# Static zero rows ahead of each pair's region, the last tile read from further back, and the imaginary product on VectorE

## The reference, cut to what matters

```python
# x: (8, 1024, 128) float32: 8 batches of 1024 tokens with 128 features
x = x + attn(layernorm(x))
x = x + moe(layernorm(x))

def attn(x):
    h = layernorm(x, gamma, beta)
    h = spiral_conv(h)          # Re(conv(h, p^t * init) + last * p^(t+1)), p one complex number per feature
    x1 = h + x
    h = layernorm(x1, gamma, beta)
    return silu(h @ w1 + b1) @ w2 + b2 + x1      # w1 128x512, w2 512x128

def moe(x):                     # 8192 tokens, 8 experts, 2 chosen for each token
    logits = x @ router.T
    top, idx = top_k(logits, 2); probs = softmax(top)
    y_e = gelu(x @ w1[e].T + b1[e]) @ w2[e].T + b2[e]   # 128 -> 256 -> 128
    return sum of probs * y_e over the two chosen experts
```

## Time and profile before

| what | value |
|---|---|
| median of 3 runs | 515.98 us (512.52 to 519.33) |
| the profiled execution | 512.49 us |
| its span, first to last instruction | 510.7 us |
| mean granted TensorE clock, share of full | 0.91 |
| busy: PE, DVE, ACT, POOL | 404.6, 350.7, 320.9, 276.0 us |
| chain that ended last | PE 46%, issue 13%, DVE 12%, POOL 8%, ACT 7%, SP's queue 4% |
| zero stores (L419, L426) | 29, of 136 KB |
| row scatters (L587), result stores (L621) | 64 and 91, on GpSimd |

### The profile page before, as it was taken

The page is one execution under the profiler, slowest core; times in us unless marked ns, Lnnn a source line. Parts: engine busy times, 40 slices in busy tenths (PEclk is TensorE's granted clock), DMA queues, the critical chain, the costliest instruction groups (busy, mean ns, idle before and its releaser), DMA issues.

```text
span 510.7 us, 11454 instructions
## 1 busy us (share of the span) xinstructions
PE 404.6 (79%) x2813; PEld 354.7 (69%) x2813; DVE 350.7 (69%) x1318; ACT 320.9 (63%) x773; POOL 276.0 (54%) x341
## 2 busy tenths in 40 slices
PE   1362379898888989888976777859998998999990
PEld 1231259686858686757765766759998998999980
DVE  7999969969987989672625555526665766676761
ACT  5690567988867797746446423436776676777750
POOL 6607662647888886855252165444544444454442
PEclk9996579999998999889979785979999999999996
DMA  8540000000111111112023125653332332333200
GB/s 264 154 120 11 0 1 1 1 1 2 45 44 35 55 34 56 49 40 77 13 87 99 33 94 185 220 175 94 99 92 82 97 97 89 95 105 101 77 6 0
DMA packets 33284, 37.43 MB, mean 73 GB/s; under 512 B 5254, under 2 KB 29331, under 8 KB 33092
## 3 DMA queue, kind: packets, MB, share of 16 engines
q1 hardware_dynamic: 27236, 23.56, 15.7%
q0 software_dynamic: 5984, 13.13, 7.5%
HBM read 19.52 MB, written 18.92 MB: 75 GB/s over the span
## 4 chain that ended last, share of the span: by engine, by line
PE 46%; issue 13%; DVE 12%; POOL 8%; ACT 7%; SPq 4%; another core or an unknown queue 1%; DMA 0%; DVEq 0%; POOLq 0%; ACTq 0%
PE up_p L1020 13%; PE up_p L1037 7%; PE down_p L1037 6%; PE down_p L862 6%; POOL sorted_rows L587 4%; PE turn_p L834 4%; ACT rows L691 2%; SPq L426 2%; DVE stats L1123 2%; PE down_p L1029 2%; ACT work L664 2%; PE up_p L848 2%; PE route_p L900 2%; PE up_p L846 2%; PE up_p L847 1%
## 5 line engine op out<-in xcount | busy, mean ns | idle before, releaser
L621 POOL DMA_INDIRECT out<-result,out_id x91 | 89.5, 984 | 108.7 <-DVE result L1498 71.0
L793 ACT ACTIVATE hid_t<-up_p 128x512 f32<-128x512 f32 x91 | 54.3, 597 | 81.4 <-PE up_p L1020 64.8
L1020 PE MATMUL up_p<-xt,work 128*128 128x128 f32 x728 | 103.1, 287 | 2.1 <-issue 1.0
L587 POOL DMA_INDIRECT sorted_rows<-rows,pos x64 | 76.8, 1199 | 39.2 <-DVE pos L1240 22.4
L1020 PEld LDWEIGHTS up_p<-xt,work 128*128 128x128 f32 x728 | 93.5, 201 | 5.2 <-issue 3.5
L808 ACT ACTIVATE work<-mw_c 128x256 f32 x182 | 65.6, 416 | 1.1 <-issue 1.1
L862 PEld LDWEIGHTS down_p<-w_sb,work 128*128 128x128 f32 x512 | 61.5, 194 | 6.4 <-issue 5.7
L862 PE MATMUL down_p<-w_sb,work 128*128 128x128 f32 x512 | 64.4, 279 | 0.5 <-issue 0.5
L651 ACT ACTIVATE work<-up_p,b_all 128x512 f32<-128x512 f32 x64 | 41.5, 682 | 22.5 <-PE up_p L848 22.5
L834 PE MATMUL turn_p<-ident,work 128*128 128x128 f32 x192 | 29.9, 307 | 29.1 <-ACT work L677 11.7
L1037 PE MATMUL down_p<-mw_sb,hid_t 128*128 x368 | 51.8, 286 | 1.0 <-issue 0.5
(11 more groups left out here) (240 smaller groups left out, 804.4 us busy)
## 6 DMA issues: line engine op xcount, KB each, us to landing
tin<-sorted_rows SPq DMA_DIRECT2D x91, 136.0 KB
resid<-in_x SPq DMA_DIRECT2D x8, 512.0 KB, 3.7
sorted_rows<-zeros SPq DMA_DIRECT2D x29, 136.0 KB, 1.8
out<-result,out_id POOLq DMA_INDIRECT x91
work<-in_mw SPq DMA_DIRECT2D x1, 1024.0 KB, 6.1
sorted_rows<-rows,pos POOLq DMA_INDIRECT x64
work<-in_w SPq DMA_DIRECT2D x1, 256.0 KB
w_sb<-in_w SPq DMA_DIRECT2D x1, 256.0 KB
```

The lines of the kernel that those rows point to most:

```text
L587: g.indirect_dma_start(sorted_dram, bass.IndirectOffsetOnAxis(pos[b % 2][:, j:j + 1], 0), rows[b % ROWBUFS][:, j, :], None).then_inc(s_sor ...
L621: g.indirect_dma_start(out_rows, bass.IndirectOffsetOnAxis(out_id[k][:, :], 0), result[k][:, :], None, bounds_check=TOKENS - 1, oob_is_err ...
L793: s_.activation(hid_t[s % 2][:, :], mid_p[s % 2][:, :], ACT.Gelu).then_inc(s_gelu, 1)
L1020: last = t.matmul(mid_p[s % 2][:, c * TILE:(c + 1) * TILE], ring[s % RING][:, c * 128:(c + 1) * 128], xt[s % 2][:, :], start=True, stop=True)
```

## The change

The zero rows get a fixed place: 128 rows in front of each region, where no token's row lies (`region_b` now starts a pair's rows 128 behind the region's start). SyncE stores all 29 tiles of zeros in a row, when the inputs' loads have been issued, and the `pads` of the tile stage, their addresses, the matmul and the addition that formed them, and the wait for them go. A pair's last tile is read from further back, so that it ends with the pair's last row: its first rows are then rows of the tile before it (or zeros), and these are masked. The table holds rows instead of tile numbers for this, and `tile_table` has two more small operations in each stage. On GpSimd `v_product` goes; the product is formed on VectorE at the end of `scans`, and the eight scatters of a batch stand in a row. Ahead of the iterations GpSimd's queue is then `decay`, `x0_scales(0)`, `x0_scales(1)`, `sort_constants`, `x1_scales(0)`, `x0_scales(2)`.

```diff
@@ sync @@
-            sp.dma_start(sorted_tiles[ZERO_TILE, :, :], zeros[:, :]).then_inc(s_zero, 16)
-
-            def pads(pairs):
-
-                sp.load(pad_sp[0:len(pairs)], pad_at[0:1, pairs[0]:pairs[-1] + 1])
-                for k in pairs:
-                    at = sp.snap(pad_sp[k - pairs[0]], min_val=0, max_val=NP * REGION - TILE)
-                    sp.dma_start(sorted_dram[bass.ds(at, TILE), :], zeros[:, :]).then_inc(s_pad, 16)
+            for k in range(NP + 1):
+                sp.dma_start(sorted_dram[k * REGION:k * REGION + TILE, :], zeros[:, :]).then_inc(s_zero, 16)
...
-                    sp.wait_ge(s_zero, 16)
-                    sp.wait_ge(s_pad, 16 * NP)
+                    sp.wait_ge(s_zero, 16 * (NP + 1))
...
-                sp.dma_start(tin[s % INS][:, :], sorted_tiles[bass.ds(at, 1), :, :].rearrange("a p r -> (a p) r"))\
+                sp.dma_start(tin[s % INS][:, :], sorted_dram[bass.ds(at, TILE), :])\
...
-                if Tail.pads <= s < Tail.pads + NP // GROUP:
-                    if s == Tail.pads:
-                        sp.wait_ge(s_pad_at, 1)
-                    k = (s - Tail.pads) * GROUP
-                    pads(range(k, k + GROUP))
@@ gpsimd @@
-                g.iota(spill_i[:, :], [[TILE, NP]], base=0, channel_multiplier=0)
+                g.iota(spill_i[:, :], [[TILE, NP]], base=TILE, channel_multiplier=0)
...
-                g.iota(row_i[:, :], [[TILE, TILES]], base=0, channel_multiplier=1)
-                g.iota(base_i[:, :], [[0, 1]], base=0, channel_multiplier=REGION // TILE)
+                g.iota(row_i[:, :], [[TILE, TILES]], base=TILE, channel_multiplier=-1)
+                g.iota(base_i[:, :], [[0, 1]], base=TILE - NOWHERE, channel_multiplier=REGION)
...
-            def v_product(b):
-                pool.wait_ge(s_vi, b + 1)
-                if b == 0:
-                    pool.wait_ge(s_tab, 1)
-                g.tensor_tensor(vi, vi, out_im, ALU.mult).then_inc(s_ti, 1)
...
-                    sort_rows(chosen_b, range(0, 2))
-                if live(b2):
-                    v_product(b2)
-                if live(chosen_b):
-                    sort_rows(chosen_b, range(2, TPB))
+                    sort_rows(chosen_b, range(TPB))
...
             decay()
             x0_scales(0)
             x0_scales(1)
-            v_product(0)
             sort_constants()
             x1_scales(0)
-            v_product(1)
             x0_scales(2)
@@ tensor @@
-                if stage == 1:
-                    t.matmul(pad_p, ones_b[:, 0:1], before[b % 2][:, :], start=True, stop=True)
@@ vector @@
                 then(d.tensor_tensor(vr, vr, out_re, ALU.mult))
+                v.wait_ge(s_vi, b + 1)
+                d.tensor_tensor(vi, vi, out_im, ALU.mult).then_inc(s_ti, 1)
...
-                if stage == 1:
-                    d.tensor_tensor(pad_at[:, :], pad_p, region_f[:, :], ALU.add).then_inc(s_pad_at, 1)
...
-                d.tensor_scalar(facts[:, 0:1], shift_n[:, :], base_t[:, :], -float(NOWHERE), ALU.add, ALU.add)
+                d.tensor_scalar(facts[:, 0:1], shift_n[:, :], float(TILE), base_t[:, :], ALU.mult, ALU.add)
...
-                chain_t(d.tensor_tensor(beyond[:, 0:n], valid_p[:, 0:n], row_n[:, 0:n], ALU.is_le))
-                d.tensor_scalar(table[0:1, low_s:high_s], fact_n[0:1, 0:n], float(ZERO_TILE), None, ALU.min)
+                d.tensor_tensor(back_n[:, 0:n], valid_p[0:1, 0:n], row_n[0:1, 0:n], ALU.subtract)
+                chain_t(d.tensor_tensor(beyond[:, 0:n], valid_p[:, 0:n], row_n[:, 0:n], ALU.is_lt))
+                chain_t(d.scalar_tensor_tensor(out=fact_n[0:1, 0:n], in0=back_n[:, 0:n], scalar=0.0, in1=fact_n[0:1, 0:n],
+                                               op0=ALU.min, op1=ALU.add))
+                d.tensor_scalar(table[0:1, low_s:high_s], fact_n[0:1, 0:n], float(ZERO_ROW), None, ALU.min)
```

More of the change, by code:

```diff
@@ L39 @@
 REGION = TOKENS + TILE
-ZERO_TILE = NP * REGION // TILE
+ZERO_ROW = NP * REGION
 PACK = 11
 GROUP = 4
-NOWHERE = 2 * ZERO_TILE
+NOWHERE = 2 * ZERO_ROW
 R_RES, R_PA, R_PB, R_ID = D, 2 * D, 2 * D + 1, 2 * D + 2
@@ L178, in block_moe_kernel @@
         ones_b = sb("ones_b", [128, 128], bf16)
-        region_i = sb("region_i", [1, NP], i32)
         all_i = sb("all_i", [1, NP], i32)
@@ L195, in block_moe_kernel @@
         row_n = sb("row_n", [128, TILES])
-        region_f = sb("region_f", [1, NP])
-        pad_at = sb("pad_at", [1, NP], i32)
+        back_n = sb("back_n", [1, TILES])
         zeros = sb("zeros", [128, ROW])
@@ L318, in block_moe_kernel @@
         s_zeros = sem("zeros_ready")
-        s_zero = sem("zero_tile_stored")
-        s_pad_at = sem("pad_rows_ready")
-        s_pad = sem("pads_stored")
+        s_zero = sem("zero_rows_stored")
         s_tc = sem("tile_counts_done")
@@ L392, in block_moe_kernel @@
             facts = 7
-            pads = 12
         def both_experts(packed):
@@ L438, in tile @@
                     sp.load(tile_sp[s // GROUP % 2][0:n], table[0:1, s:s + n])
-                at = sp.snap(tile_sp[s // GROUP % 2][s % GROUP], min_val=0, max_val=ZERO_TILE)
+                at = sp.snap(tile_sp[s // GROUP % 2][s % GROUP], min_val=0, max_val=ZERO_ROW)
                 after(sp, s_o, s - INS + 1)
-                sp.dma_start(tin[s % INS][:, :], sorted_tiles[bass.ds(at, 1), :, :].rearrange("a p r -> (a p) r"))\
+                sp.dma_start(tin[s % INS][:, :], sorted_dram[bass.ds(at, TILE), :])\
                     .then_inc(s_in[s % INS], 16)
             tile_sp = [[sp.alloc_register(f"tile_sp{q}{k}") for k in range(GROUP)] for q in range(2)]
-            pad_sp = [sp.alloc_register(f"pad_sp{k}") for k in range(GROUP)]
             sp.wait_ge(s_table, 1)
@@ L536, in sort_constants @@
                 g.tensor_copy(slot_n[:, :], slot_i[:, :])
-                g.tensor_scalar(first_n[0:1, :], slot_i[0:1, :], 1.0, float(NOWHERE), ALU.mult, ALU.add)
-                g.tensor_copy(region_f[:, :], region_i[:, :])
+                g.tensor_scalar(first_n[0:1, :], slot_i[0:1, :], float(TILE), float(NOWHERE), ALU.mult, ALU.add)
                 g.tensor_copy(row_n[:, :], row_i[:, :])
```

3 lines of the change are left out of this document (removed).

## The result

The changed kernel takes 493.75 us (median of 4 runs, 490.28 to 495.79) where the kernel before, run beside it, takes 517.62 (512.52 to 519.33): a ratio of 0.954, 95% interval 0.949 to 0.959. That is 24 us, where 14.9 were forecast; 493.75 lies just under the range of 494 to 512. The profiled executions, 490.28 and 512.49 us, are 22.2 apart. 12.4 of these lie ahead of the first tile turn (271.91 before, 259.53 after), 9.8 behind it.

The account below looks back on a forecast made before the run. GpSimd was taken to bound iterations 3 to 5, TensorE the tiles from 343 us. Terms 3.8 + 1.2 + 0.9 + 1.3 + 8.0 - 0.3 = 14.9 us off 515.98 gave 501; range 494 to 512.

Parts of the forecast that it names:

- Prologue, 3.8: Ahead of the batches: moving the product off GpSimd readies x0_scales(2) sooner and removes ScalarE's wait, 3.8 us gained.
- Iterations 3 and 4, 1.2 + 0.9 = 2.1: Batches: earlier scatters and scales gain 1.2 us in iteration 3; a shorter ScalarE delay gains 0.9 in iteration 4.
- VectorE is late next: Iteration 3: scales come 2.5 us earlier, but VectorE then limits, so only 1.2 us is gained.
- Iteration 5, 1.3: Batches, iteration 5: ScalarE's extra delay behind the sum before its x1 norm goes, 1.3 us gained.
- Iterations 6 and 7, nothing: Last batch iterations: they have no product, so no gain was counted.
- The table, -0.3: Before the first tile: two more small table operations delay TensorE, a loss of 0.3 us.
- Tile stage, 8.0: Tiles 9 to 17: load waits and stops, 8.8 us beyond 2.06 a tile, mostly go; 8.0 us gained.
- Rival 2: Tile stage: stops are not the stores' doing, only load waits go, 5.7 of 8; 503 us, chance 0.17.
- 1: Batches: VectorE is the pacemaker, GpSimd's relief buys nothing, all eight products count; 515 us, chance 0.12.
- 3: Early zero stores: their backlog starves the engines between 33 and 55 us, costing 20; 521 us, chance 0.05.
- 4: Batches: VectorE's product holds scatters as long as GpSimd's did; iterations 3 to 5 lose 3.4; 504.5 us, chance 0.06.
- tile 17 within 22 us of tile 9: Tile stage sign: tile 17's first product some 22 us behind tile 9's or less, 16.5 if whole.

Follow-up runs that it names:

- e3: Kernel before with x0_scales(2) moved ahead of v_product(1) in GpSimd's queue; first sum 1.63 us earlier, time unchanged.
- e4: Kernel before with the product on VectorE for batches 0 and 1 alone, GpSimd keeping the other six; 1.2% faster (0.983 to 0.992).
- e5: Kernel before with eight more TensorE transposes ahead of its x2 norm wait in iterations 1 to 5; 0.8% faster (0.985 to 0.998).
- e7: Changed kernel with 28 zero stores to fixed addresses of unread rows, four ahead of each of tiles 12 to 18; 0.959 of the kernel before.
- e2: Kernel before with the static zero stores and the last tile moved back alone, product still on GpSimd; ratio 0.988.
- e12: Changed kernel with one more 128x1024 VectorE instruction per batch, 1.2 us each; first tile turn 9.1 us later, no total time given.
- e10: Changed kernel with each of the 29 early zero stores issued twice, the second to unread rows; first sum at 83.70 us, no total time given.
- e8: Changed kernel with SyncE waiting at tile 12 for the last batch's tile counts, no added stores; 0.959 of the kernel before.
- e9: Changed kernel with the edits of e7 and e8 together, fixed-address stores and SyncE's wait; 0.965 of the kernel before.

## Why the prediction came out as it did

**Direction** was right in both halves, and so was the mechanism of the prologue and of the exchange between GpSimd and VectorE. The sum was 9 us too small by the medians (24 against 14.9), 7.3 by the profiled executions (22.2). By its own terms, against the profiled executions:

- Prologue, 3.8: the first sum came 4.85 earlier. The reason was right in its place and half of it in its form: e3 shows that the order alone gives 1.6. What the term left out is what follows: iteration 1 took 1.6 back, with a TensorE wait of 2.54 us and a fall of the clock near 98 us. By the second sum 3.3 are left, 4.2 where the clock does not fall.
- Iterations 3 and 4, 1.2 + 0.9 = 2.1: measured 2.65 + 0.72 = 3.4. The step that failed is the working of a gain from the waits of a single iteration. With GpSimd's product the round was 26.6 us (e4, e5), and 28.20 and 24.94 were that round twice, unevenly cut; after the change the two take 49.8 together. "VectorE is late next" was right: the new periods are VectorE's.
- Iteration 5, 1.3: measured 4.1. 1.7 of it are the scheduling (25.74 to 24.08), 2.4 the clock, which e5 gives back alone. The step that failed is the clock, which the sum left at nothing: the term counted a wait by its length, but behind the 2.22 us standing of TensorE the clock fell to half as well. The split rests on e5's one profiled execution.
- Iterations 6 and 7, nothing: measured 1.7, of which 1.3 the clock.
- The table, -0.3: the first turn comes 1.37 us behind the last sum, as before (1.36). Nothing.
- Tile stage, 8.0: measured 9.8 in the profiles, 5.5 of it up to turn 20. Behind turn 20 the rest varies from 157.4 to 163.8 over the kernels with the static zeros and from 157.6 to 166.0 over those without; the 4.4 us between these two executions belong to no part of the change. The waits for loads, 5.7, went as forecast, but a stop of 6.25 us stands in their place, and tiles 9 to 17 went only from 29.1 to 27.4. Two steps failed. The reading: 25.3 us are seven tiles, not eight; at 2.06 a tile that leaves 10.9 of waits and stops in them, and 12.6 in eight tiles, not 8.8. And the cause: the stops were not the stores' (e7 has their traffic and takes no more time, and the changed kernel has none and stops for 6.25 us). Rival 2 named this rightly, and 5.5 is near its 5.7, but the match is partly luck: with the pads the waits for loads sum to 5.7 to 9.6 us, while turn 20 comes at 75.6 to 77.3 whatever they are; without pads it comes at 70.2 to 72.6.

So the batches were undersized by 5.5 us (12.4 against 6.9), most of it the clock and the round, and these carry the miss. The zeros' half is 9.8 in the profiles but some 6 in the timed runs (e2), near rival 2.

**The rivals.** 1: VectorE is the pacemaker, but only once the round of 26.6 through GpSimd is gone; e12 shows it at nearly full price, and still the exchange paid. 3: false, even doubled (e10). 4: false. The scatter at 130.48, beside the new product, took 0.96. But the ones that start within a scan or within the subtraction L1160 took 3.01 and 1.86. The Trainium skill (SBUF — State Buffer, Who interferes with whom) infers that a tensor_tensor leaves descriptor generation alone; the scatter at 133.01, started 0.18 us into a tensor_tensor and 1.86 long, is against that, and the one at 130.48, started 0.07 ahead of one, is not held.

**The signs named in the prediction.** Seen: no wait for the product, the rotation near 71, eight scatters in a row that end 4.7 us behind the sum in place of 7.3, waits near 1.5 us for the x1 scales, no wait for a load. Missing: tile 17 within 22 us of tile 9, and no stop over 3 us.

## What to carry to other kernels

Where two engines alternate as the limit, size a change by the period over two or more iterations, and by what is in the round that sets it, not by the waits of one iteration: two iterations of 28.2 and 24.9 were one round of 26.6, twice. Then look at what TensorE does in the waits that go: a standing of 2.2 us here cost 2.4 us more through the clock. Before a stretch is turned into time per tile, count the tiles in it. Stores whose addresses are loaded into registers held SyncE's queue longer here than fixed ones (31.3 us against 21.3 for 28), so what can be made static should leave a queue on which loads wait, even if its traffic is free.

## What the runs showed that was not expected

- Fillers that only keep TensorE busy gained 0.8% on the kernel before (0.985 to 0.998) and nothing on the changed one.
- Stores with a register address took SyncE 31.3 us for 28, with the loads between them, fixed ones 21.3, in kernels alike but for the registers and their loads.
- A program shifted by 32 to 48 instructions in the prologue moved a stop 250 us later from 8.3 us to 5.5 or to another tile, and left the stage's length alone; but the same stop also shrank or moved when only SyncE's program was changed (e8, e9). The Trainium skill (Runtime: NRT & Kernel Launch, Instruction fetch mechanics) calls the cost of crossing from one block of code to the next "mostly hidden". No run here shows a fetch holding an engine, and none excludes it.
